# The first batch of a decoder layer: a scale per quarter of the query weight, weights, units and softmax interleaved

## The reference, cut to what matters

```python
# x: (8, 256, 512); 32 query heads and 8 key/value groups of 64
x = x + attention(layernorm(x), Wq, Wk, Wv, Wo, bo)
x = x + xattn(ctx_2048, ctx_2048, layernorm(x), ssm_kernel, D, 8)
x = x + ffn(layernorm(x), w_gate_up, w_proj)        # ternary weights

def attention(h, Wq, Wk, Wv, Wo, bo):
    q, k, v = heads(h @ Wq), heads(h @ Wk), heads(h @ Wv)
    q, k = rope(q), rope(k);  k, v = repeat(k, 4), repeat(v, 4)
    scores = (q @ k.T - abs(i - j) * slope[head]) / 8
    scores = 30 * tanh(scores / 30), masked causally
    return merge(softmax(scores) @ v) @ Wo + bo
```

## Time and profile before

| what | value |
|---|---|
| median of 3 runs | 1391.8 us |
| the profiled execution | 1391.77 us, its span 1390.0 us |
| TensorE busy | 1235.1 us, 89% of the span |
| VectorE, ScalarE, GpSimd busy | 68%, 43%, 43% |
| mean granted TensorE clock | 0.955 of full speed |
| chain that ended last | TensorE 68%, VectorE 12%, issue 7% |

### The profile page before, as it was taken

The page is one execution under the profiler, slowest core; times in us unless marked ns, Lnnn a source line. Parts: engine busy times, 40 slices in busy tenths (PEclk is TensorE's granted clock), DMA queues, the critical chain, the costliest instruction groups (busy, mean ns, idle before and its releaser), DMA issues.

```text
span 1390.0 us, 20096 instructions
## 1 busy us (share of the span) xinstructions
PE 1235.1 (89%) x7264; PEld 833.5 (60%) x7264; DVE 940.8 (68%) x1253; ACT 603.4 (43%) x712; POOL 593.5 (43%) x496
## 2 busy tenths in 40 slices
PE   2483497999999999999999868999879999999996
...
GB/s 267 82 120 67 150 145 65 125 108 118 107 147 124 113 120 99 147 124 120 114 85 148 123 169 84 152 138 152 38 0 2 16 16 1 15 15 16 1 16 31
DMA packets 130201, 127.97 MB, mean 92 GB/s; under 512 B 31750, under 2 KB 89382, under 8 KB 130150
## 3 DMA queue, kind: packets, MB, share of 16 engines
...
## 4 chain that ended last, share of the span: by engine, by line
PE 68%; DVE 12%; issue 7%; ACT 6%; POOL 3%; DMA 3%; SPq 0%; DVEq 0%; ACTq 0%; POOLq 0%
PE bank L681 11%; PE bank L727 8%; PE bank L728 8%; PE bank L541 8%; PE bank L542 8%; PE bank L543 8%; PE bank L746 4%; PE bank L747 4%; PE bank L608 3%; PE bank L590 2%; PE bank L591 2%; ACT region_c L841 2%; DMA wffn<-wo 2%; DVE ctx L1033 2%; ACT rsum L808 1%
## 5 line engine op out<-in xcount | busy, mean ns | idle before, releaser
L727 PE MATMUL bank<-h_hi,guT 128*128 128x256 f16 x1024 | 226.9, 274 | 1.4 <-DVE h_lo L1314 1.4
L728 PE MATMUL bank<-h_lo,guT 128*128 128x256 f16 x1024 | 226.9, 274 | 0.0
L541 PE MATMUL bank<-hT_hi,w_hi 128*128 128x256 f16 x640 | 176.9, 276 | 29.7 <-DVE hT_lo L999 15.5
L1413 POOL TENSOR_TENSOR parts<-parts 128x512 f32<-128x512 f32 x80 | 127.9, 1603 | 156.7 <-DVE parts L1012 149.6
L608 PE MATMUL bank<-region_c,v 128*128 128x512 f32 x256 | 138.9, 625 | 44.7 <-DVE ctx L1033 44.7
L542 PE MATMUL bank<-hT_lo,w_hi 128*128 128x256 f16 x640 | 176.7, 276 | 0.0
L543 PE MATMUL bank<-hT_hi,w_lo 128*128 128x256 f16 x640 | 176.6, 276 | 0.0
L1418 POOL TENSOR_SCALAR_AFFINE_SELECT region_c<-region_c 128x512 f32<-128x512 f32 x128 | 101.7, 817 | 150.0 <-ACT region_c L844 150.0
L681 PE MATMUL bank<-kv,toep 128*128 128x288 f32 x640 | 157.1, 409 | 8.9 <-POOL kv L1479 7.1
L681 PEld LDWEIGHTS bank<-kv,toep 128*128 128x128 f32 x640 | 122.4, 192 | 43.5 <-POOL kv L1479 7.6
L841 ACT ACTIVATE region_c<-bank,cap_scale 128x1536 f32<-128x1536 f32 x64 | 98.7, 1542 | 70.8 <-PE bank L591 69.7
...
## 6 DMA issues: line engine op xcount, KB each, us to landing
unit_halves<-halves SPq DMA_DIRECT2D x80, 256.0 KB, 2.3
q_both<-unit_halves SPq DMA_DIRECT2D x64, 256.0 KB, 3.1
...
toep<-kernel_padded SPq DMA_DIRECT2D x32, 256.0 KB, 3.8
...
```

What stands on the lines that cost most here:

```text
L541: pe.matmul(dst, lh, rh, start=first and k == 0, stop=False)
L727: pe.matmul(dst, guT[:, k, col:col + P], h3_hi[:, p, k, :], start=(k == 0), stop=False)
L728: mm = pe.matmul(dst, guT[:, k, col:col + P], h3_lo[:, p, k, :], start=False, stop=(k == DB - 1))
L1413: pool.tensor_tensor(slot[:, 0], slot[:, 0], slot[:, 1], ALU.add).then_inc(unit_summed, 1)
```

## The change

All of it stands in what is done before the first pass of the loop over batches, but for the numbering of units.

1. Wq gets a scale per quarter (I_Q is four indices). `cap_scale` and `dist_scale` have four columns, and the bias rows are laid quarter by quarter (`lay_bias`).
2. The maximum over partitions goes by TensorE: VectorE multiplies the identity with the column of row maxima (`square`), TensorE multiplies a matrix of ones with it (`top`), VectorE reduces the 128 columns of the result, which stand in every partition.
3. The second unit of keys is number 5 instead of 1. The first two units are stored both and then placed both. Weights, units and softmax steps of batch 0 are interleaved by hand, engine by engine (`first_batch`): two softmax steps start with five units made.
4. Wo is loaded once, six pieces into the place of raw Wq, two slots behind the place where each is split to, and two into `wffn`. VectorE subtracts w_lo (`low_wo`), ScalarE scales and rounds in one instruction (`high_wo`), both between units of batch 1. The last quarter of Wq is scaled in place and split by ScalarE and GpSimd.
5. The first feed-forward share is loaded ahead of all units and rounded in step 2.
6. The bias rows are 6 instead of 32, and fills of the 26 others go; the second scores product takes 70 rows instead of 128.

```diff
+KEY_UNITS = {0: 0, 5: 1}
+QUERY_UNITS = {n: g for g, n in enumerate(n for n in range(UNITS) if n not in KEY_UNITS)}
+UNIT_OF_KEYS = {j: n for n, j in KEY_UNITS.items()}
+UNIT_OF_QUERIES = {g: n for n, g in QUERY_UNITS.items()}
...
+        wo_slots = region_o[:].rearrange("p (c r n) -> p c r n", c=O_PIECES, n=D)
+        wo_raw = ([wo_slots[:, c + O_SHIFT] for c in range(O_PIECES - O_SHIFT)]
+                  + [wffn[:, 2 * c + 2:2 * c + 4, :] for c in range(O_SHIFT)])
...
-                load_piece(FIRST[I_Q] + c, wq_raw[:, :, q_cols[c]], wq.rearrange("(k p) n -> p k n", p=P)[:, :, q_cols[c]])
             sp.dma_start(key_bias_s[bias_rows], key_bias).then_inc(consts_in, 16)
-            sp.wait_ge(cleared, 1)
-            sp.dma_start(q_high[2 * HALF:2 * HALF + BIAS_ROWS], query_bias).then_inc(bias_in, 16)
+            load_piece(I_Q[1], wq_raw[:, :, q_cols[1]], wq_t[:, :, q_cols[1]])
...
             sp.wait_ge(t_filled, TT)
...
+            for n in range(2):
+                store_unit(0, n)
+            for n in range(2):
+                place_unit(0, n)
+            for n in range(2, UNITS):
+                if n == 4:
+                    sp.wait_ge(kpad_step, 2)
+                    sp.dma_start(kpad_d, kpad).then_inc(kpad_stored, 16)
+                if n == 6:
+                    sp.wait_ge(w_lo_done, SCALES - 2)
+                    sp.wait_ge(w_apart, 2)
+                if n == UNITS - 1:
+                    sp.wait_ge(w_rounded, 1)
+                for c in range(2 * (n - 6), 2 * (n - 5)) if n >= 6 else ():
+                    sp.dma_start(wo_raw[c], wo.rearrange("(k p) n -> p k n", p=P)[:, o_rows[c], :]).then_inc(wo_in[c], 16)
                 store_unit(0, n)
...
+            def top(n):
+
+                where, part = TOP_AT[n]
+                square, ones = square_and_ones(n)
+                pe.wait_ge(squared, n + 1)
...
+                pe.matmul(bank[:, where, part * P:(part + 1) * P], ones, square, start=True, stop=True).then_inc(top_filled, 1)
+
+            def first_batch():
+                pe.wait_ge(ident_in, 16)
+                for i in range(TT):
+                    turn(0, i)
+                pe.wait_ge(fills, 3)
+                top(I_K)
+                top(I_Q[0])
+                pe.wait_ge(w_lo_done, I_K + 1)
+                project(0, 0, True)
+                pe.wait_ge(w_lo_done, I_Q[0] + 1)
+                project(0, 1, True)
+                top(I_Q[1])
+                project(0, 2, True)
+                pe.wait_ge(w_lo_done, I_Q[1] + 1)
+                project(0, 3, True)
+                top(I_V)
+                scores(0, 0, True)
+                project(0, 4, True)
+                top(I_Q[2])
+                pe.wait_ge(w_lo_done, I_V + 1)
+                project_values(0, 0, True)
+                scores(0, 1, True)
+                project_values(0, 1, True)
+                project(0, 5, True)
+                top(I_Q[3])
+                for step in range(2, STEPS):
+                    if step == 2:
+                        pe.wait_ge(w_lo_done, I_Q[2] + 1)
+                    elif step == 4:
+                        pe.wait_ge(w_apart, 2)
+                    if step < 6:
+                        project(0, step + 4, True)
+                    if step < NG:
+                        scores(0, step, True)
+                    values(0, step - 2, True)
+                    if step == NG:
+                        top(I_O)
+                        pe.wait_ge(tanh_done, NG)
+                        for i in range(TT):
+                            turn(1, i)
...
+            def high_wo(c):
+                if c == 0:
+                    act.wait_ge(wscale_step, SCALE_STEPS * (I_O + 1))
+                    act.wait_ge(wo_in[0], 16)
+                if c >= O_SHIFT:
+                    act.wait_ge(wo_lo_done, c - O_SHIFT + 1)
+                act.activation(wo_hi[c], wo_raw[c], ACT.Copy, scale=wscale[:, I_O:I_O + 1]).then_inc(wo_hi_done, 1)
...
+                high_weight(I_Q[1])
+                high_unit(0, 2, True)
+                high_weight(I_V)
+                soften(0, 0)
+                high_unit(0, 3, True)
+                high_weight(I_Q[2])
+                act.wait_ge(fills, 3)
+                take_values(0, 0)
+                high_unit(0, 4, True)
+                soften(0, 1)
+                take_values(0, 1)
+                high_unit(0, 5, True)
+                raw, hi, _ = WEIGHTS[I_Q[3]]
+                act.wait_ge(wscale_step, SCALE_STEPS * (I_Q[3] + 1))
+                act.activation(raw, raw, ACT.Copy, scale=wscale[:, I_Q[3]:I_Q[3] + 1]).then_inc(w_hi_done, 1)
+                act.wait_ge(w_hi_done, I_Q[3] + 1)
+                act.copy(hi, raw).then_inc(w_apart, 1)
...
+            def square(n):
+
+                dve.wait_ge(wmax_done, n + 1)
+                dve.tensor_scalar(square_and_ones(n)[0], ident_s[:], wmax[:, n:n + 1], None, ALU.mult).then_inc(squared, 1)
...
+                dve.wait_ge(top_filled, n + 1)
+                dve.tensor_reduce(wtop[:, one], bank[:, where, part * P:(part + 1) * P], AX_X, ALU.max).then_inc(wscale_step, 1)
...
+            def low_wo(c):
+                dve.wait_ge(wo_hi_done, c + 1)
+                dve.scalar_tensor_tensor(wo_lo[c], wo_raw[c], wscale[:, I_O:I_O + 1], wo_hi[c], ALU.mult, ALU.subtract
+                                         ).then_inc(wo_lo_done, 1)
...
+                find_scale(I_K)
+                largest(I_Q[0])
+                find_scale(I_Q[0])
+                low_weight(I_K)
+                for i in range(TT):
+                    low(0, i)
+                low_weight(I_Q[0])
+                largest(I_Q[1])
...
+                rotate(0, 0, True)
+                rotate(0, 1, True)
+                find_scale(I_Q[1])
+                lay_bias(0)
+                rotate(0, 2, True)
+                low_unit(0, 0)
+                low_unit(0, 1)
+                low_weight(I_Q[1])
+                largest(I_V)
+                low_unit(0, 2)
+                find_scale(I_V)
+                rotate(0, 3, True)
+                largest(I_Q[2])
+                low_weight(I_V)
+                rotate(0, 4, True)
+                low_unit(0, 3)
+                find_scale(I_Q[2])
+                lay_bias(1)
...
+                largest(I_Q[3])
+                low_unit(0, 4)
+                low_weight(I_Q[2])
+                rotate(0, 5, True)
+                find_scale(I_Q[3])
+                rotate(0, 6, True)
+                low_unit(0, 5)
+                for step in range(2, STEPS):
+                    if 3 <= step < 6:
+                        rotate(0, step + 4, True)
+                    normalise(0, step - 2, True)
+                    if step < 6:
+                        low_unit(0, step + 4)
+                    if step < Q_PIECES:
+                        lay_bias(step)
+                    for c in {4: (0, 1), 5: (2, 3), 6: (4, 5), 7: (6, 7)}.get(step, ()):
+                        largest_of_wo(c)
+                    if step == 6:
+                        prepare(1, TT)
+                    if step == 7:
+                        prepared(1)
+                    if step == NG:
+                        find_scale(I_O)
...
+                        for i in range(TT):
+                            low(1, i)
+                    if step == NG + 1:
+                        low_wo(0)
+                        find_thresholds(0)
+                low_wo(1)
+                for n in range(EARLY):
+                    rotate(1, n)
+                    if n + O_SHIFT < O_PIECES:
+                        low_wo(n + O_SHIFT)
+                    if n:
+                        low_unit(1, n - 1)
+                    if n == EARLY - 1:
+                        for i in range(TT):
+                            output(0, i)
...
```

546 lines of the change are left out of this document (265 added, 281 removed).

## The result

The changed kernel takes 1340.45 us, the median of 4 runs (1337.12 to 1341.89); the kernel before took 1391.67 in the same job (4 runs, 1391.26 to 1392.36). The ratio is 0.9628, 95% interval 0.961 to 0.9646: 51 us less, where 52.6 were forecast (1339). The profiled execution is the slowest of the four: 1341.89 us, span 1340.2, mean clock 0.967. Single runs of one kernel differ by up to 5.6 us here, so medians of kernels less than 3 us apart don't tell them apart.

What follows compares the result with a forecast made beforehand. Ahead of batch 1 TensorE idled 91.7 us, waiting for VectorE's contexts, with VectorE waiting for Wo. Gains of 45.9 (batch 1's start), 4.3 (second scores) and 2.4 (clock) sum to 52.6: 1391.8 to 1339 us, range 1324 to 1356.

Steps and rivals of the forecast that it cites:

- the 15 pieces: Batch 1's first seven units and batch 0's eight output pieces on TensorE: 39.2 us as before, with no wait.
- Key scale: Scale of the key weight Wk at the start, maximum by TensorE: ready at 14.5 us instead of 21.8, gain 7.3.
- First scores: Batch 0's first scores product on TensorE, behind the first placed units: starts at 42.7 us instead of 78.9.
- transfer: From a unit's low part to its placed rows, through store and placing: 6 us, or 8 for two units in a row.
- The stretch with weights and units mixed: VectorE's busy stretch from 34.4 us: 26.9 us of work to quarter 3's scale at 61.3, then scores 4 at 80.8.
- Steps 4 to 7: Batch 0's later softmax steps: scores 6 at 99.7 us, scores 7 at 107.5, batch 1's first unit at 130.
- the cycle: Scores, softening, sums, normalise, low part and transfer, each unit needing an earlier step: 17 to 19 us for two steps.
- To the second scores: From the end of the 15 pieces to batch 1's second scores: 9.2 us instead of 13.5, gain 4.3.
- A: Rival: VectorE's 100 us of work sets batch 1's start, at 107 to 120 us; priced at 1327 us, chance 0.22.
- B: Rival: the cycle is longer, each of steps 2 to 7 by 2.5 us, 15 us in all; 1354 us, chance 0.18.
- C: Rival: the matrix path of the maxima is no faster than GpSimd, key scale 7 us later; 1346 us, chance 0.09.
- D: Rival: stores of units 6 to 9 wait behind Wo loads, six steps of 22 us; 1423 us, chance 0.04.

Runs made afterwards that it cites:

- e4_warm: The changed kernel with matmuls added whose result nothing reads, 48 ahead of unit 3 and 16 ahead of the first values projection: 1335.95 us.
- e1_gpsimd_max: The changed kernel with the maximum over partitions of all seven weight maxima taken by GpSimd again, not by TensorE and VectorE: 1376.92 us.

## Why the prediction was right, point by point

The total was 1.5 us off, and what carries it is as forecast: batch 1's first unit 45.8 us earlier, the 15 pieces unchanged, the waits for contexts and for Wo gone. No experiment undoes the interleaving or the single load of Wo alone, so their shares rest on the trace. The points, in the prediction's order, forecast against measured:

| mark | forecast | measured |
|---|---|---|
| key scale | 14.5 | 15.04 |
| first scores | 42.7 | 44.12 |
| quarter 3's scale | 61.3 | 65.9 |
| scores 4 | 80.8 | 84.86 |
| scores 6 | 99.7 | 102.56 |
| batch 1's first unit | 130 | 130.10 |
| from there, 15 pieces | 39.2 | 39.4 |
| from there to second scores | 9.2 | 10.8 |

*Key scale.* Right to 0.5: Wk's reduction started at 8.37 instead of 7.77 (0.6), the float product took 0.64 and not 0.4, square and reduction 0.29 each.

*First scores.* 1.4 late, through unit 3, which stands ahead of the scores and ran at the low clock but for its last matmuls (39.06 to 44.06). I had counted on a transfer that ends last, but TensorE's order does: no wait stands at the first scores. The transfer itself was sized right: in e4_warm unit 3 ends at 41.8, TensorE idles 0.7 us, and the scores start at 42.75. (The sum's own steps, 34.4 and 8, give 42.4 and not 42.7.)

*The stretch with weights and units mixed.* The term that was mis-sized. From the end of low unit 0 (35.07) to quarter 3's scale it is 30.8 us where I had 26.9; and the items that I listed for it add up to 26.3, so 0.6 of the 26.9 had no source. The values projection took 5.3 us at the low clock, twice its 2.75 at the full one, and VectorE waited 2.70 us for unit 5 behind it. e4_warm shows it: with the clock up for unit 3 and for the projection the scale comes 5.1 us earlier, and that wait is 0.19. Another 1.1 us were lost at 34.99, where the low part of unit 1 took 1.75 us instead of 0.68. GpSimd summed unit 2 meanwhile:

```profile
34.99 1.75 DVE L1254 TENSOR_TENSOR halves<-parts,halves 128x512 f16<-128x512 f32 x1
34.55 1.64 POOL L1559 TENSOR_TENSOR parts<-parts 128x512 f32<-128x512 f32 x1 [1.71 <-DVE parts L1113]
```

*Steps 4 to 7.* From scores 4 to batch 1's first unit I had 47.8 and 1.4 for a contended standardisation; it took 45.2. From scores 4 to VectorE's work on the sums of step 4 (110.24) I had 27.4 and it took 25.4, of which scores 4 to 6 are 17.7 instead of 18.9, still inside the cycle's 17 to 19. From there on I had 21.8 and it took 19.9, mostly because the standardisation took 1.00 us, with GpSimd idle beside it. So the 1.4 for contention was in the wrong place. The Trainium skill's warning on shared interfaces ("GPSIMD Engine Reference", 8 Key points) was not put to the test at the standardisation. At 34.99, with two inputs in SBUF, the trace agrees with it (1.75 us against 0.68). These 4 us covered the stretch before: the 130 was met by two errors that cancel, not by a sound sum, and by luck in the execution too, since the same code gave 127.95 to 130.41.

*Batch 1's units.* As forecast, with no wait. VectorE even idles 5.1 us ahead of the last turn.

*To the second scores.* The 2.64 us of waiting was priced (2.7); the values projection behind it at the low clock for most of its length (4.15 instead of 2.6) was not. The gain there was 2.7 instead of 4.3. The 2.4 for the clock of the second scores and the unit behind was 2.3 (228.57 to 234.91 before, 180.30 to 184.39 after).

*Rivals.* A is out: VectorE's work up to batch 1's first unit is 93.5 us, near the 100 of the sum, but it idles for the other 36.6, of which 16.7 are waits for ScalarE's sums. (The middle of A's range is 1322.5; its price of 1327 was not that.) B is out: batch 1's first unit would be at 145. C is out at the key scale: from maximum to scale the matrix path takes 4.4 us and not 11. What is real in C is the ones product behind a unit: VectorE waits 2.21 us for that of Wv at 44.33, which the sum had as 2. C's 7 us are not what going back to GpSimd costs in the new order either: 36 (e1_gpsimd_max), the gaps around seven reductions. D appears in small: stores shortly behind loads land 1.1 to 2.9 us later, and the steps don't fall to the old pace.
